# An order list of its own for the first batch of a fused mixer, feed-forward and attention kernel

## The reference

```
x = x + mixer(layernorm(x))       # RWKV-6 like: low-rank token mixing, r/w/k/v/g projections, decay scan, gate
x = x + ffn(layernorm(x))         # 256 -> 1024, butterfly, gelu, butterfly, 1024 -> 256
x = x + attention_block(layernorm(x))   # 16 heads of 16, rotary, causal, then an MLP
x = x + ffn(layernorm(x))         # the same ffn weights again
```

```
h = einsum(x, W_exp) + b_exp
h = butterfly(h, up_weights, 1024)        # 10 stages
h = gelu(h + up_bias)
h = butterfly(h, down_weights, 1024)      # 10 stages
y = einsum(h, W_con) + b_con + down_bias
```

## Time and profile before

| what | us |
|---|---|
| median of 3 runs | 1728.87 |
| lowest and highest | 1727.68, 1731.99 |
| the profiled execution's own time | 1731.26 |
| its span, first to last instruction | 1729.4 |
| mean granted TensorE clock | 0.981 |

### The profile page before, as it was taken

The page is one execution under the profiler, slowest core; times in us unless marked ns, Lnnn a source line. Parts: engine busy times, 40 slices in busy tenths (PEclk is TensorE's granted clock), DMA queues, the critical chain, the costliest instruction groups (busy, mean ns, idle before and its releaser), DMA issues.

```text
span 1729.4 us, 47107 instructions
## 1 busy us (share of the span) xinstructions
PE 1634.0 (94%) x20436; PEld 1186.2 (69%) x20436; DVE 951.8 (55%) x1978; ACT 722.3 (42%) x1510; POOL 671.0 (39%) x851
## 2 busy tenths in 40 slices
PE   6579999999999999999999999999999999999998
PEld 3467468865688557884588746886478845777577
DVE  6864657356553657446573565636565365734621
ACT  4433462334632454234623346324552346333441
POOL 5633335343532426333362434424263242723110
PEclk9889999999999999999999999999999999999999
DMA  5110000000000000000000000000000000000000
GB/s 185 51 50 13 3 14 3 1 26 14 3 2 13 13 14 3 2 25 2 15 3 1 26 14 3 2 1 26 14 3 1 14 13 2 3 2 0 2 13 13
DMA packets 20413, 26.22 MB, mean 15 GB/s; under 512 B 1488, under 2 KB 18800, under 8 KB 20208
## 3 DMA queue, kind: packets, MB, share of 16 engines
q1 hardware_dynamic: 19872, 22.16, 3.9%
q0 software_dynamic: 336, 1.05, 0.2%
HBM read 19.01 MB, written 4.19 MB: 13 GB/s over the span
## 4 chain that ended last, share of the span: by engine, by line
PE 74%; DVE 13%; ACT 6%; issue 4%; POOL 1%; DMA 1%; SPq 0%; DVEq 0%; POOLq 0%; ACTq 0%
PE ring L1593 20%; PE ring L1607 18%; PE ring L1579 5%; PE ring L1760 4%; PE attn_out L1787 4%; PE ring L1539 4%; PE ring L1711 4%; DVE maxes L1334 3%; PE ring L1646 3%; PE ring L1733 2%; PE ring L1531 2%; PE ring L1616 2%; PE ring L1739 2%; DVE mix L1223 2%; DVE x_z_xb L1177 1%
## 5 line engine op out<-in xcount | busy, mean ns | idle before, releaser
L1334 DVE TENSOR_REDUCE maxes<-ring 128x2 f32<-128x1024 f32 (+5 forms) x290 | 197.5, 739 | 82.5 <-PE ring L1739 82.0
L758 POOL TENSOR_TENSOR rstd<-mean_var,eps_and_power 128x2 f32<-128x2 f32 x96 | 19.5, 203 | 468.6 <-DVE mean_var L1171 468.6
L1607 PE MATMUL ring<-w_down,big 128*128 128x256 f32 x784 | 175.9, 379 | 0.0
L1607 PEld LDWEIGHTS ring<-w_down,big 128*128 128x128 f32 x784 | 147.3, 190 | 19.6 <-issue 0.4
L810 POOL TENSOR_TENSOR big<-big,decay_blocks 128x256 f32<-128x256 f32 x192 | 141.7, 767 | 41.6 <-issue 36.8
L781 POOL TENSOR_TENSOR mix<-mix,z_t 128x512 f32<-128x512 f32 x80 | 85.8, 1101 | 119.2 <-DVE mix L1223 119.2
L1760 PE MATMUL ring<-big 32*64 32x128 f32 (+3 forms) x2048 | 125.6, 458 | 1.7 <-DVE big L1366 0.9
L1025 ACT ACTIVATE big<-ring,up_bias 128x256 f32<-128x256 f32 x196 | 82.3, 471 | 103.5 <-PE ring L1593 103.5
L1267 DVE TENSOR_TENSOR big<-big,decay_blocks 128x256 f32<-128x256 f32 x192 | 123.7, 670 | 1.0
L1593 PE MATMUL ring<-maxes,w_mlp 128*128 128x256 f32 x512 | 118.2, 385 | 0.0
L1593 PE MATMUL ring<-v,w_up 128*128 128x256 f32 x512 | 117.1, 389 | 0.0
(11 more groups left out here) (202 smaller groups left out, 3323.8 us busy)
## 6 DMA issues: line engine op xcount, KB each, us to landing
x_in<-in_x SPq DMA_DIRECT2D x8, 512.0 KB, 3.8
delta<-in_x SPq DMA_DIRECT2D x7, 512.0 KB, 3.9
out<-x_z_xb SPq DMA_DIRECT2D x7, 512.0 KB, 3.0
w_mlp<-in_wm SPq DMA_DIRECT2D x2, 1024.0 KB, 6.2
w_mlp<-in_w_exp_t SPq DMA_DIRECT2D x1, 1028.0 KB, 9.9
v_ones<-in_w_con SPq DMA_DIRECT2D x1, 1024.0 KB, 9.9
w_mlp<-in_low_up SPq DMA_DIRECT2D x1, 1016.0 KB, 6.7
w_attention<-in_low_down SPq DMA_DIRECT2D x1, 1016.0 KB, 8.2
```

The source lines that it names most:

```text
L1334: nc.vector.tensor_reduce(maxes[:, t % 2, qt, 32 * gs[0] + row:32 * gs[-1] + row + 1:32], banks[:, first:last, lo:hi], AX_X, ALU.max).then ...
L1607: ins = mm(ps[:, a * D:(a + 1) * D], gelu(b, tag, m, t)[:, a * P:(a + 1) * P], wd[:, m, :], start=(m == 0), stop=(m == NF - 1))
```

## The change

The functions `high_steps`, `low_steps`, `woven`, `folded_into` and `first_half` go. In their place `opening()` returns the first batch's steps as a written list, up to and with the steps of batch 1 that are set into batch 0's attention. It holds the same steps as before. No operand, tile or instruction of a step differs. The order differs in these places:

- `xl 0` stands ahead of `hd 0 0`, and `blend 1 0` ahead of both; `fin 2` ahead of `hd 0 3`; `hd 1 4`, `hu 0 0` and the rest of `hd 1` ahead of `blend 4 0`; `w 0` ahead of the second half of `x5`.
- `hu 2 5` to `hu 2 7` stand ahead of `r 2` and `r 3`; `upb` behind `A 0 0`; the `v` products are split around `A 0 1`, `A 1 1` and level 2.
- `hd 2 0` stands in level 1, `hd 2 1` to `hd 2 3` in levels 6 and 7, `hd 2 4` between `o 0` and `o 1`, the rest behind `norm N`, with `tw` and `biases` between. `g` goes from ahead of level 5 to behind `A 7 0`.
- `o 1` stands ahead of `norm N 0`; `up F 0 0` and `0 1` ahead of `zt F 1`.
- In the attention of batch 0: `xl 1` of batch 1 goes from behind `proj 0 1 0` to behind `half 0 1 high`; `x5 1 0` of batch 1 into the low rotation; `zt B 1` ahead of `roundq low`; `fold 0 1 high` ahead of `half 0 0 high`.

```diff
-def woven(main, extra, weights):
-    share = [weights.get(s[1:3], weights.get(s[1], 0.0)) for s in main]
...
-def folded_into(main):
...
+def opening():
+
+    return [
+        (0, "norm", "A", 0), (0, "norm", "A", 1), (0, "zt", "A", 0), (0, "zt", "A", 1), (0, "delta"), (0, "mix0"),
+        (0, "low", "up", 0), (0, "low", "up", 1), (0, "blend", 1, 0), (0, "low", "up", 2), (0, "low", "up", 3),
+        (0, "xl", 0), (0, "low", "up", 4), (0, "low", "up", 5), (0, "hd", 0, 0), (0, "hd", 0, 1), (0, "hd", 0, 2),
+        (0, "xl", 1), (0, "x5", 1, 0), (0, "x5", 2, 0), (0, "mix", 1, 0), (0, "x5", 1, 1), (0, "x5", 2, 1),
+        (0, "blend", 1, 1), (0, "mix", 1, 1), (0, "fin", 2), (0, "blend", 2, 0), (0, "mix", 2, 0),
+        (0, "blend", 2, 1), (0, "hd", 0, 3), (0, "mix", 2, 1), (0, "hd", 0, 4), (0, "hd", 0, 5), (0, "hd", 0, 6),
+        (0, "hd", 0, 7), (0, "fin", 3), (0, "wa"), (0, "k", 0, 0), (0, "hd", 1, 0), (0, "hd", 1, 1), (0, "hd", 1, 2),
+        (0, "k", 0, 1), (0, "hd", 1, 3), (0, "x5", 0, 0), (0, "x5", 3, 0), (0, "x5", 4, 0), (0, "blend", 0, 0),
+        (0, "mix", 0, 0), (0, "blend", 3, 0), (0, "mix", 3, 0), (0, "mix", 4, 0), (0, "k", 1, 0), (0, "hd", 1, 4),
+        (0, "hu", 0, 0), (0, "hd", 1, 5), (0, "hd", 1, 6), (0, "k", 1, 1), (0, "hd", 1, 7), (0, "w", 0),
+        (0, "x5", 0, 1), (0, "blend", 4, 0), (0, "x5", 3, 1), (0, "x5", 4, 1), (0, "blend", 0, 1), (0, "mix", 0, 1),
...
+        (0, "hu", 2, 5), (0, "hu", 2, 6), (0, "hu", 2, 7), (0, "r", 2), (0, "r", 3), (0, "A", 0, 0), (0, "upb"),
+        (0, "A", 1, 0), (0, "v", 0, 0), (0, "v", 0, 1), (0, "A", 0, 1), (0, "hd", 2, 0), (0, "A", 1, 1),
+        (0, "v", 1, 0), (0, "A", 2, 0), (0, "A", 2, 1), (0, "v", 1, 1), (0, "A", 3, 0), (0, "A", 3, 1), (0, "ga", 0),
+        (0, "ga", 1), (0, "A", 4, 0), (0, "A", 4, 1), (0, "rows"), (0, "A", 5, 0), (0, "A", 5, 1), (0, "place"),
+        (0, "A", 6, 0), (0, "A", 6, 1), (0, "A", 6, 2), (0, "hd", 2, 1), (0, "A", 6, 3), (0, "hd", 2, 2),
+        (0, "A", 7, 0), (0, "g"), (0, "A", 7, 1), (0, "hd", 2, 3), (0, "A", 7, 2), (0, "kt", 0), (0, "A", 7, 3),
+        (0, "kt", 1), (0, "kt", 2), (0, "kt", 3), (0, "s", 0), (0, "s", 1), (0, "s", 2), (0, "o", 0),
+        (0, "hd", 2, 4), (0, "o", 1), (0, "norm", "N", 0), (0, "norm", "N", 1), (0, "hd", 2, 5), (0, "hd", 2, 6),
+        (0, "tw", 0), (0, "hd", 2, 7), (0, "tw", 1), (0, "biases"), (0, "tw", 2), (0, "ogt", 0), (0, "ogt", 1),
+        (0, "tw", 3), (0, "fin", 0), (0, "ao", 0), (0, "norm", "F", 0), (0, "ao", 1), (0, "norm", "F", 1),
+        (0, "xbf"), (0, "clear_maxes"), (0, "fin", 1), (0, "zt", "F", 0), (0, "up", "F", 0, 0), (0, "up", "F", 0, 1),
+        (0, "zt", "F", 1), (0, "up", "F", 0, 2), (0, "up", "F", 0, 3), (1, "norm", "A", 0), (0, "up", "F", 1, 0),
...
+        (0, "proj", 0, 0, 0), (0, "proj", 0, 1, 0), (0, "norm", "B", 1), (0, "z2", 1), (0, "rot", 0, 0, "low"),
+        (0, "rot", 0, 1, "low"), (1, "x5", 1, 0), (0, "fold", 0, 0, "low"), (0, "half", 0, 0, "low"),
+        (0, "zt", "B", 1), (0, "roundq", 0, "low"), (0, "fold", 0, 1, "low"), (0, "half", 0, 1, "low"),
+        (0, "roundk", 0, "low"), (1, "x5", 1, 1), (1, "blend", 1, 0), (1, "mix", 1, 0), (1, "blend", 1, 1),
+        (1, "mix", 1, 1), (0, "proj", 0, 0, 1), (0, "proj", 0, 1, 1), (0, "rot", 0, 0, "high"),
+        (0, "rot", 0, 1, "high"), (0, "fold", 0, 0, "high"), (0, "fold", 0, 1, "high"), (0, "half", 0, 0, "high"),
+        (0, "roundq", 0, "high"), (0, "S", 0, "c"), (0, "vb", 0), (0, "half", 0, 1, "high"), (1, "xl", 1),
...
 def whole_program():
 
-    ahead = [step for step in merged_steps(None, None, 0) + attention_steps(-1, 0) if step[0] == 0]
-    first = merged_steps(0, None, 1 if B > 1 else None)
-    until = first.index((0, "zt", "F", 0))
-    o = folded_into(ahead + first[0:until]) + first_half(first[until:], attention_steps(0, 1 if B > 1 else None))
+    o = opening()
```

More of the change, by code:

```diff
@@ L267, in whole_program @@
 def whole_program():
-    ahead = [step for step in merged_steps(None, None, 0) + attention_steps(-1, 0) if step[0] == 0]
-    first = merged_steps(0, None, 1 if B > 1 else None)
-    until = first.index((0, "zt", "F", 0))
-    o = folded_into(ahead + first[0:until]) + first_half(first[until:], attention_steps(0, 1 if B > 1 else None))
+    o = opening()
     for b in range(1, B - 1):
         o += merged_steps(b, b - 1, b + 1) + attention_steps(b, b + 1)
[L275 to L278, removed]
+    o += last_mixer(merged_steps(B - 1, B - 2, None)) + attention_steps(B - 1, None)
+    return o + kept_back(merged_steps(None, B - 1, None))
 ROUNDS = "abc"
```

19 lines of the change are left out of this document (11 added, 8 removed), and 20 rows, old and new, of the table at.

## The result

| what | us |
|---|---|
| before, median of 6 runs (lowest, highest) | 1731.22 (1727.68, 1735.91) |
| changed, median of 6 runs (lowest, highest) | 1717.22 (1712.43, 1720.05) |
| ratio, with its 95% interval | 0.9918 (0.9900 to 0.9937) |
| the profiled execution's own time, its span, its mean clock | 1717.02, 1715.2, 0.985 |

The account below looks back on a forecast made before the run. TensorE was taken to bound the body, VectorE to be the full engine of the opening. Terms -0.8+2.4+1.5+1.6+1.7+2.4+2.3 made 11.1, less 0.6 gave a gain of 10.5: median 1718.4 us, range 1711.5 to 1726.

Parts of the forecast that it names:

- the first term: Start to level 2 of the scores: a loss of 0.8 us, from an early slip of 3.4 partly paid back.
- The gate: `g` moved behind `A 7 0`: VectorE's wait and gate work leave the path to level 5, a gain of 2.4 us.
- Norm N: First state copy to the end of the second norm: statistics of both halves come before both norms, a gain of 1.6 us.
- The wait ahead of the second `zt F`: Two `up F` steps fill TensorE's wait of 2.81 us, a gain of 1.7 us.
- the clock there: At `up F`, with the wait filled, TensorE's granted clock stays full instead of half, a gain of 2.4 us.
- The rotations: Batch 0's first rotations, up to its attention scores: gain 2.3 us, between 3.6 at full clock and 1.0 if it falls.
- Rival (a): The clock stays half at `up F` and `proj`: gain only 6.8 us, 1722.1; chance 0.15.
- (b): The early slip stays and the gate holds VectorE as well: gain 4.3 us, 1724.6; chance 0.15.
- (c): The early slip in the opening costs nothing: gain 14.3 us, 1714.6; chance 0.12.
- (d): More folding steps meet GpSimd at 0.83 us each, making it slower, at worst 14.4 us, 1743.3; chance 0.05.
- (e): The change does nothing, since TensorE bounds everything; chance 0.03.

Follow-up runs that it names:

- blend_behind: The changed kernel with `blend 1 0` put back behind `hd 0 2`; 1716.97 us, one time.
- r_back: The changed kernel with `r 2` and `r 3` put back between the last folding steps of `hu 2`; 1714.90 us, one time.
- gate_back: The changed kernel with `g` put back behind `rows` and ahead of level 5; 1722.62 us beside 1732.63, one time each.
- norm_back: The changed kernel with `norm N 0` put back ahead of `o 1`; 1719.61 us, one time.
- up_behind: The changed kernel with `up F 0 0` and `0 1` put back behind `zt F 1`; 1719.27 us, one time.
- the halves: Two kernels, with the new order only up to `fin 1` or only behind it, the old order elsewhere; 1722.41 and 1727.18 us against 1727.35.
- late_half: The old order up to `fin 1`, the new order behind it; 1727.18 us against 1727.35 before, ratio 0.9985.
- the second trace of the changed kernel: The changed kernel profiled again, nothing altered; median 1716.58 us against 1730.12 before, ratio 0.9920.
- loads_sp: The changed kernel with the five bias and table loads issued by SyncE instead of GpSimd; 1719.68 us, ratio 0.9950 to before.

## Why the prediction was right, and where it was wrong

**The step that failed** is the first term, "its slip of 3.4 reaches `r 0`", and with it the sum of -0.8. It was mis-sized in three places, which the runs tell apart. GpSimd's first downward product was 1.83 late, not 3.4; `blend_behind` shows that some 1.6 of it is the blend ahead of the folding steps, so the queue slide that I worked out (22.3) was right and the later folding steps among the mixes cost next to nothing. Then 1.83 did not reach `r 0`, which came only 0.55 late: from the product to `r 0` every trace with the changed order and the loads on GpSimd took 12.71 to 12.73, and both of the order of before 13.99. (The 0.55 itself is no more than executions differ by: `r 0` came between 54.52 and 55.84 in the changed order, and at 55.29 and 55.33 in that of before.) I had let GpSimd's chain carry the slip; but the `r` eviction stands behind ScalarE's scalings and these behind VectorE's folding steps. VectorE began stage 1 of `hu` 0.82 sooner than before (46.99, not 47.81), since `hu 0 0` stands ahead of `blend 4 0` and stage 0 was done at 46.96, not 47.78, and so it had more done when GpSimd's loads and tree came. Last, the payback by `r 2` and `r 3` was 0.86, not 2.4 (`r_back`). What made the term a gain all the same is one that I had counted small: the eight bias sums stood ahead of the first score copy with 1.99 (62.98 to 64.89), two of them 0.83 and 0.80 long beside GpSimd's scaling of k. Behind the copy and clear of GpSimd they take 0.63. The rows of the kernel before:

```profile
62.98 1.99 DVE L1395 TENSOR_TENSOR up_bias<-w_mlp,cols 128x1 f32<-128x1 f32 x8
64.89 1.01 DVE L1251 COPY_PREDICATED score_blocks<-masks,ring 128x256 f32<-128x256 uint16 x2
```

So the first copy came 2.34 sooner, with the last `hu` only 0.3 sooner; the products and `hd 2 0` behind it take 0.5 back. One sentence beside this term is wrong in its arithmetic: a price that is the same before and after, like the 1.6 of the step held by the loads, does not enter the sum, which is a difference. The 0.6 for code loads and drops of clock came from no row, and no run shows a part of it that is code loads.

**The gate** was right in kind: 3.33 in the profiled pair for 2.4, and 1.4 to 3.0 by the nine other traces with the gate there, so that the difference is within what executions differ by. I had let TensorE's pause ahead of level 5 bound it at 1.8 to 3.0; `gate_back` has 1.30 and 1.73 back in full in VectorE's queue, so the pause did not bind. TensorE still pauses at level 5, for GpSimd's scaled k, but VectorE has the steps before it to do and copies at 77.94 without idle time:

```profile
78.15 0.71 PE L1645 MATMUL ring<-big 128*16 128x16 f32 x64 [2.41 <-POOL big L809]
```

VectorE did wait for ScalarE ahead of the gate, one of the signs that I named as speaking against me, but 0.56 where up to 3 was feared, and level 5 to the first state copy still gained 2.07 for 1.5.

**Norm N** was right: 1.48 for 1.6, the length 6.97 for "some 7", shown by `norm_back` (1.87 lost). **The wait ahead of the second `zt F`** and **the clock there** were right: 4.71 for 4.1 (1.9 and 2.8 for 1.7 and 2.4), shown three times (`up_behind`, and the halves). **The rotations** were right in mechanism, and the full-clock end was right: `late_half`, with full clock at `proj`, gains 3.65 where I had 3.6, and the second trace of the changed kernel 3.62. With 0.50 in 148 to 150 the first gains 2.05 where I had 1.0. That the mean of 2.3 comes so near to one trace is luck, since the stretch has either end and the list doesn't choose it.

**What I did not foresee** is the size of what the clock takes back later. My term "drops of clock that fall elsewhere" was 0.6 together with code loads. In the profiled pair it was 6.0 lost to the clock by 276 us and 4.8 won back by the end, of which the clock shows 2.2, a second fall of the clock being another sign that I had named. The two nearly cancel in that pair: the stretches gain 15.46, 4.4 more than my 11.1 (2.6 of it by the first term, 0.9 by the gate, 0.6 each by level 5 to the state copy and by `up F`, less 0.1 and 0.25), and the end keeps 14.2.

**The rivals.** Rival (a), the clock stays half, is out at `up F`; at `proj` it is true in the first trace of the changed kernel and out in the second. (b) is out: the slip was 0.55 at `r 0`, and the wait ahead of the gate was 0.56. (c), the slip costs nothing, has the gain that came, 14.3, by another road: the slip exists, and terms that I had smaller pay for it. (d), slower by the shared use of SBUF, is out in sum, though its price is real: the eight folding steps at 46.99 took 9.69 instead of 7.85, beside GpSimd's products, loads and tree; without the loads (`loads_sp`) they take 8.15. (e) is out.

**What stays open** is why the clock falls in the attention of batch 0 in every kernel but the one before. The pause at 159 was tried: with it at 0.53 the clock fell all the same, and the kernel before has it at 1.58 without a fall. That kernel has its 6.8 us at half clock ahead of the first scores instead, where the stretches put them down to the rotations. With one trace of the kernel before it isn't even shown that it always keeps its clock there.

## What to carry to other kernels

Follow a slip step by step through the queue that the late instruction really stands in: a chain that was 1.8 late on one engine was 0.55 late at the eviction that I had hung on it. Count small vector instructions that stand ahead of the first use of a result with their co-running price; eight of 128x1 took 1.99, more than the gate's wait of 1.30. And judge moves of this size by their stretch in the trace, in more than one trace: the halves are 9.5 and 7.5 us ahead where they act and gained 0.2 and 4.9 in the total, with the clock falling differently behind them, while the same order took 10.64 and 12.29 for the same stretch in two executions.

## What the runs showed of the hardware

A VectorE folding step with two operands in SBUF that began while GpSimd issued the second of its five loads ended 0.08 to 0.18 us after the last was issued, after 2.12 us, in the kernel before and in the changed one. Steps beside the first of these issues took 0.47 to 0.49. When SyncE issued the same loads this hold was gone (the eight steps 8.15 instead of 9.69, with the same steps in the same order). That run moves the transfers too, so that it is the issuing rests on where the hold ended. The Trainium skill (SBUF — State Buffer, Who interferes with whom) infers that descriptor writing leaves such an instruction alone; in this kernel the traces and `loads_sp` say otherwise.

The same 1967 matmuls of the attention took 116.35 us at a granted clock of 1.00 and 122.34 at 0.94, with TensorE's busy time 5.92 apart of those 5.99. That is more than any one move of the list gained, and the same kernel profiled twice differed there by 2.2. In all thirteen traces the length follows the time at half clock: none, 116.35; 6.8 us, 118.45; 10.2 us, 119.97 to 120.44; 13.7 us, 121.56 to 122.34.
